# A conditioned transformer layer on one core: the output gate moved to the head of its slot, the first twelve attention slots taken by couples, and the inverse RMS spread through DRAM instead of by transpositions

## The reference, cut to what matters

```python
x = layernorm(x) * w + b + tanh(cond @ lin_w.T + lin_b)      # x: 128 sequences x 64 tokens x 256
x = x * w + b
rms = lambda v: v * rsqrt(mean(v * v, axis=-1) + 1e-6)
x = x + a_alpha * attention(a_gamma * rms(x) + a_beta)        # 16 heads of 16
h = f_gamma * rms(x) + f_beta
x = x + f_alpha * (silu(h @ gate_w.T) * (h @ hidden_w.T) @ out_w.T + out_b)   # hidden 1024
```

## Time and profile before

| | |
|---|---|
| median of 3 runs | 1007.26 us (1006.86 to 1007.68) |
| the profiled execution's own time | 1006.64 us |
| its span | 1004.8 us |
| TensorE busy | 943.0 us, 94% of the span |
| VectorE, ScalarE, GpSimd busy | 719.9, 623.0, 581.7 us |
| mean granted clock of TensorE | 0.993 |

### The profile page before, as it was taken

One profiled execution on the slowest core, in us unless ns is written; L12 is line 12 of the kernel. 1 busy time (PEld: TensorE's weight loads), 2 busy tenths in 40 slices (PEclk: granted clock), 3 DMA queues, 4 the chain that ended last, 5 costly groups with the idle time before them and its releaser, 6 DMA issues.

```text
span 1004.8 us, 28386 instructions
## 1 busy us (share of the span) xinstructions
PE 943.0 (94%) x11164; PEld 899.6 (90%) x11164; DVE 719.9 (72%) x1349; ACT 623.0 (62%) x1775; POOL 581.7 (58%) x531
## 2 busy tenths in 40 slices
PE   5566999999999999999999999999999999999998
PEld 5445899999999999999999999999999999999997
DVE  6656777777777777777777777777777776766655
ACT  4555766676566567656656765665667567666432
POOL 4556666757465665746566664656666565544320
PEclk9899999999999999999999999999999999999999
DMA  6000001000010100000010000001000000000000
GB/s 236 17 22 2 23 12 33 6 30 13 13 32 12 33 11 23 12 14 32 12 34 12 23 12 16 30 12 33 12 22 13 12 13 12 12 12 12 12 12 22
DMA packets 20931, 23.34 MB, mean 23 GB/s; under 512 B 1216, under 2 KB 20288, under 8 KB 20800
## 3 DMA queue, kind: packets, MB, share of 16 engines
q1 hardware_dynamic: 20800, 21.54, 6.6%
HBM read 13.15 MB, written 8.39 MB: 21 GB/s over the span
## 4 chain that ended last, share of the span: by engine, by line
PE 89%; DVE 4%; issue 3%; POOL 2%; ACT 1%; DMA 0%; SPq 0%; DVEq 0%; ACTq 0%; POOLq 0%
PE psum L293 18%; PE psum L295 17%; PE psum L294 17%; PE psum L507 6%; PE psum L506 6%; PE psum L505 6%; PE psum L432 5%; PE psum L408 4%; PE psum L448 4%; PE psum L342 2%; PE psum L323 2%; PE psum L501 1%; DVE late L721 1%; PE psum L331 1%; PE psum L335 1%
## 5 line engine op out<-in xcount | busy, mean ns | idle before, releaser
L293 PE MATMUL psum<-xf_hi,ffn_hi 128*128 128x256 f32 x1024 | 289.8, 283 | 2.3 <-ACT probsT L905 1.6
L295 PE MATMUL psum<-xf_hi,ffn_lo 128*128 128x256 f32 x1024 | 285.9, 279 | 0.0
L294 PE MATMUL psum<-xf_lo,ffn_hi 128*128 128x256 f32 x1024 | 285.8, 279 | 0.0
L897 ACT ACTIVATE probs<-psum,least 128x64 f32<-128x64 f32 x976 | 215.7, 354 | 56.6 <-DVE least L632 55.3
L293 PEld LDWEIGHTS psum<-xf_hi,ffn_hi 128*128 128x128 f32 x1024 | 192.2, 188 | 3.6 <-issue 2.6
L1091 POOL TENSOR_TENSOR probs<-probs,inv_sum 128x512 f32<-128x512 f32 x128 | 134.8, 1053 | 104.2 <-DVE inv_sum L653 103.4
L295 PEld LDWEIGHTS psum<-xf_hi,ffn_lo 128*128 128x128 f32 x1024 | 192.4, 188 | 0.0
L294 PEld LDWEIGHTS psum<-xf_lo,ffn_hi 128*128 128x128 f32 x1024 | 192.0, 187 | 0.0
L926 ACT ACTIVATE prod_hi<-late 128x512 fp32r<-128x512 f32 x128 | 83.9, 656 | 136.1 <-DVE late L711 135.9
L507 PE MATMUL psum<-prod_hi,ffn_lo 128*128 128x256 f32 x512 | 143.1, 280 | 0.0
L703 DVE SCALAR_TENSOR_TENSOR late<-tanh,psum 128x512 f32<-128x512 f32 x128 | 87.4, 683 | 77.7 <-ACT tanh L920 77.7
(11 more groups left out here) (106 smaller groups left out, 2217.9 us busy)
## 6 DMA issues: line engine op xcount, KB each, us to landing
out_t_dram<-x_res SPq DMA_DIRECT2D x31, 256.0 KB, 2.2
xin<-x_dram SPq DMA_DIRECT2D x15, 512.0 KB, 4.0
w_raw<-attn_w_dram SPq DMA_DIRECT2D x1, 1024.0 KB, 7.0
x_res<-gate_w_dram SPq DMA_DIRECT2D x1, 1024.0 KB, 9.6
late<-hidden_w_dram SPq DMA_DIRECT2D x1, 1024.0 KB, 11.6
w_raw<-out_w_dram SPq DMA_DIRECT2D x1, 1024.0 KB, 6.4
xin<-x_dram SPq DMA_DIRECT2D x2, 256.0 KB, 2.9
k_heads<-mod_w_dram SPq DMA_DIRECT2D x1, 320.0 KB, 4.7
```

Source lines behind the costliest of these rows:

```text
L293: pe.matmul(out, stat_hi, mov_hi, start=first, stop=False)
L294: pe.matmul(out, stat_hi, mov_lo, start=False, stop=False)
L295: return pe.matmul(out, stat_lo, mov_hi, start=False, stop=last)
L897: op = act.activation(probs[g % 2][:, h * SEQ:(h + 1) * SEQ], scores[g % 2][:, h // 2, h % 2], ACT.Exp, bias=least[g % 2][:, h:h + 1], sca ...
```

## The change

Three edits. **Output gate:** `gate_ffn` moves on VectorE from behind the sums and scalings of its slot S1 to its head, ahead of `mean_squares_out`. **Couples:** `wide(g)` now holds for odd sequences too, so in slots 0 to 11 VectorE centres both sequences of a couple and inverts both sums in the even slot, ScalarE takes two wide exponentials one after the other, and GpSimd normalises both at the head of the even slot. **Inverse RMS:** from group 3 (`ROWS_FROM`) on, `spread_inverses` is gone. SyncE stores `mean_sq` to a small DRAM tensor, waits for it, and loads it back with every partition getting the same row of up to 512 numbers (`send_inverses`); `scale_a` and `scale_f` read that row from SBUF, and `scale_f` goes first. `turn_squares` reads every second column, so that the row comes out in the order of the tokens.

```diff
+ROWS_FROM = FFN_AT // PSEQ
...
         def wide(g):
-            return g < FFN_AT and g % 2 == 0
+            return g < FFN_AT
...
+        def token_cols(grp, ap, i):
+            return ap[:].rearrange("p (t i) -> p i t", i=2)[:, i] if grp >= ROWS_FROM else ap[:, i * P:(i + 1) * P]
...
+            def send_inverses(grp):
+                which = slice(0 if is_part(grp + 2) else 1, 2 if is_part(grp - 2) else 1)
+                sp.wait_ge(inv_made, grp + 3)
+                sp.dma_start(inv_dram[grp % 2].rearrange("(w p i) -> p w i", w=2, i=2)[:, which],
+                             mean_sq[:].rearrange("p (w i) -> p w i", i=2)[:, which]).then_inc(inv_stored, 16)
+                if grp >= ROWS_FROM + 2:
+                    sp.wait_ge(scaled_a, min(grp + 1, NPART))
+                    sp.wait_ge(scaled_f, grp - 3)
+                sp.wait_ge(inv_stored, 16 * (grp - ROWS_FROM + 1))
+                cols = slice(which.start * PART, which.stop * PART)
+                sp.dma_start(inverse[grp % 2][:, cols], inv_dram[grp % 2:grp % 2 + 1, cols].partition_broadcast(P)
+                             ).then_inc(row_loaded, 16)
...
+                if s % PSEQ == 1 and s // PSEQ >= ROWS_FROM and is_group(s // PSEQ):
+                    send_inverses(s // PSEQ)
...
-                if j == 2 and is_part(grp + 2):
+                if j == 2 and grp < ROWS_FROM:
                     pe.wait_ge(scaled_a, grp + 3)
-                if j == 2 and is_part(grp - 2):
-                    pe.wait_ge(scaled_f, grp - 1)
+                    if is_part(grp - 2):
+                        pe.wait_ge(scaled_f, grp - 1)
...
-                if j == 2 and is_group(grp) and s >= 0:
+                if j == 2 and 0 <= grp < ROWS_FROM:
                     spread_inverses(grp)
...
+                if j == 1 and 0 <= grp - 4 < NPART - 1:
+                    gate_ffn(grp - 4)
+                if j == 1 and grp - 4 == NPART - 1:
+                    finish_last(grp - 4)
                 if j == 1 and is_group(grp):
                     mean_squares_out(grp)
...
+                    if s == 0:
+                        scale_a(1)
+                    for g in (s, s + 1):
+                        if is_seq(g) and wide(g):
+                            invert_sums(g)
...
                 if j == 0 and is_part(grp + 2):
                     make_residual(grp + 2)
+                if j == 2 and is_part(grp - 2):
+                    scale_f(grp - 2)
                 if j == 2 and s >= 0 and is_part(grp + 2):
                     scale_a(grp + 2)
-                if j == 2 and is_part(grp - 2):
-                    scale_f(grp - 2)
-                if is_seq(s):
+                if is_seq(s) and not wide(s):
                     invert_sums(s)
```

More of the change, by code:

```diff
@@ L136, in conditioned_block @@
         prod_lo = [sb(f"prod_lo{i}", [P, BLK], F32R) for i in range(2)]
+        inv_dram = nc.dram_tensor("inv_dram", [2, 2 * PART], F32).ap()
+        inverse = [sb(f"inverse{i}", [P, 2 * PART]) for i in range(2)]
         gated_f = late[:, 0:KT * PART].rearrange("p (k c) -> p k c", k=KT)
@@ L173, in conditioned_block @@
         out_mm, gated_f_made, y_made = sem("out_mm"), sem("gated_f_made"), sem("y_made")
+        inv_stored, row_loaded = sem("inv_stored"), sem("row_loaded")
         last_gated, last_made = sem("last_gated"), sem("last_made")
@@ L330, in turn_squares @@
                     for i in range(2):
-                        mm = pe.transpose(norm_bank[:, i * P:(i + 1) * P], square_sum_a[:, i * P:(i + 1) * P], ident[:])
+                        mm = pe.transpose(norm_bank[:, i * P:(i + 1) * P], token_cols(grp, square_sum_a, i), ident[:])
                 if is_part(grp - 2):
@@ L670, in mean_squares_out @@
                 dve.wait_ge(ms_mm, grp + 3)
-                if grp >= -1:
+                if grp > ROWS_FROM:
+                    dve.wait_ge(inv_stored, 16 * (grp - ROWS_FROM))
+                elif grp >= -1:
                     dve.wait_ge(inv_spread, grp + 2)
@@ L677, in mean_squares_out, with scale_by_rms @@
                 dve.tensor_scalar(mean_sq[:, cols], square_mean[:, cols], RMS_EPS, None, ALU.add).then_inc(ms_out, 1)
[L679 to L682, removed]
+            def scale_by_rms(normed, grp, cols):
+                if grp < ROWS_FROM:
+                    dve.wait_ge(inv_spread, grp + 3)
+                    row = norm_bank[:, cols]
+                else:
+                    dve.wait_ge(row_loaded, 16 * (grp - ROWS_FROM + 1))
+                    row = inverse[grp % 2][:, cols]
+                return dve.tensor_tensor(normed[:], normed[:], row.unsqueeze(1).broadcast_to([P, KT, PART]), ALU.mult)
             def scale_a(m):
-                dve.wait_ge(inv_spread, m + 1)
                 dve.wait_ge(gamma_a, m + 1)
-                scale_by_rms(normed_a, 0).then_inc(scaled_a, 1)
+                scale_by_rms(normed_a, m - 2, slice(0, PART)).then_inc(scaled_a, 1)
             def scale_f(m):
-                dve.wait_ge(inv_spread, m + 5)
                 dve.wait_ge(gamma_f, m + 1)
-                scale_by_rms(normed_f, PART).then_inc(scaled_f, 1)
+                scale_by_rms(normed_f, m + 2, slice(PART, 2 * PART)).then_inc(scaled_f, 1)
             def ffn_split_lo(m):
@@ L780, in _ @@
                                 centre(g)
+                    if s == 0:
[3 more added lines that the diff above has]
+                            invert_sums(g)
                 if s == FIRST_SLOT + 2:
                     scale_a(0)
-                if s == 0:
-                    scale_a(1)
                 if j == 0 and is_part(grp + 2):
                     make_residual(grp + 2)
+                if j == 2 and is_part(grp - 2):
+                    scale_f(grp - 2)
                 if j == 2 and s >= 0 and is_part(grp + 2):
                     scale_a(grp + 2)
-                if j == 2 and is_part(grp - 2):
-                    scale_f(grp - 2)
-                if is_seq(s):
+                if is_seq(s) and not wide(s):
                     invert_sums(s)
@@ L794, in _ @@
                     attended_lo(grp - 1)
-                if j == 1 and 0 <= grp - 4 < NPART - 1:
-                    gate_ffn(grp - 4)
-                if j == 1 and grp - 4 == NPART - 1:
-                    finish_last(grp - 4)
                 if j == 3 and is_part(grp - 1):
@@ L883, in score_minima_found @@
                 if wide(g):
-                    act.wait_ge(scores_read, g + 1)
+                    act.wait_ge(scores_read, g + 2)
             def exponentials(g):
@@ L979, in _ @@
                     exponentials(s)
+                    if wide(s + 1):
+                        exponentials(s + 1)
                 if s == 0:
@@ L1007, in _ @@
                     half_tanh(f)
-                if s % 2 == 0 and is_seq(s + 1):
+                if s % 2 == 0 and is_seq(s + 1) and not wide(s + 1):
                     exponentials(s + 1)
@@ L1110, in _ @@
                     apply_beta_a(1)
+                for g in (s, s + 1):
+                    if s % 2 == 0 and is_seq(g) and wide(g):
+                        normalise_probs(g)
+                if s == 0:
                     split_lo_a(1)
```

2 lines of the change are left out of this document (1 added, 1 removed).

## The result

The change makes the kernel slightly slower. Its median is 1011.92 us (1006.68 to 1015.48, 16 runs) against 1007.45 us of before (1005.09 to 1009.07, 16 runs) beside it; the ratio is 1.0043, interval 1.0029 to 1.0056. The forecast was 983.8. The profiled execution's span is 1010.1 us, its own time 1011.9.

A forecast was written before the change was run, and what follows sets the result against it. After about 100 us only TensorE's work and stops were taken to count. Gate -16.8, transpositions -7.0 and couples +0.3 gave -23.5, so 983.1 from the profiled 1006.64, and a median of 983.8 us; range 978 to 997.

The forecast's parts named there:

- Output gate, -16.8: End of S1: `down` no longer waits for the output gate, 28 x 0.60 = 16.8 us gained.
- +0.3 us, between -2 and +3: Couples in slots 0 to 11: gains and delays nearly cancel, +0.3 us, between -2 and +3.
- The end of slot 11 within 2 us: Sign for the couples: slot 11 ends within 2 us of before.
- 2.4 + 2.6 and 0.3, 5.3: Inverse's way through DRAM: two DMAs of 2.4 and 2.6 us plus 0.3 for three semaphores, 5.3 us.
- The upper bound of 8.1: Inverse's way through DRAM: estimate from above, each small piece twice as dear, 5.2 + 2.9 = 8.1 us.
- The point where lateness starts to cost, 6.8: Steady groups: both DMAs may take 6.8 us before TensorE stands still; about 7.0 in odd groups.
- rival C: Row too late: each us beyond 6.8 costs one in 27 groups, slower from 7.7; chance 0.05 below break-even, 0.11 above.
- The sign that was named: Forecast wrong if the wait for `inverse` exceeds 1.6 us; then TensorE waits for `att_lo` in S3.
- Transpositions, 7.0 of 11.6: Groups 3 to 33: 116 transpositions gone save 11.6 us of TensorE, of which 7.0 us arrive.
- The odd groups' chain: Minima, merges and VectorE work up to `turn_squares` in odd groups leave even groups' S2 gaining only some 0.05 us.
- The read with a stride at 0: `turn_squares` reading every second column: 0 or a doubling worth 12 us; taken as 0.
- The scalings from SBUF: Two SBUF operands beside GpSimd: at worst `scale_a` takes 1.76 us, 1.07 more, inside the 1.6 us slack.

The follow-up runs named there:

- gate_alone: The kernel before with only the output gate moved to the head of its slot: 989.11 us, ratio 0.9823.
- dram_alone: The kernel before with only the inverse RMS row through DRAM from group 3 on: 1010.27 us, ratio 1.0037.
- stale_row: gate_and_dram with each scaling using the previous group's row, so it never waits for its own (wrong results): 987.28 us, ratio 0.9807.
- gate_and_dram: The changed kernel without the couples (gate first, rows through DRAM): 1003.07 us, ratio 0.9967; run again on a third chip, 1002.65 us.
- hybrid: gate_and_dram with rows through DRAM only in groups 3 to 29, TensorE spreading inverses in groups 30 to 33: 997.68 us, ratio 0.9916.
- down_first: hybrid with scalings behind `att_lo`, statistics merges in S0 of odd groups, and `down` ahead of the values' projection in S2: 986.90 us, ratio 0.9792.
- the two runs on the second chip: gate_and_dram with the output's store moved to S3, 1011.68 us; gate_and_dram with the statistics merges moved to S0 of odd groups, 1007.38 us.

## Why the prediction was wrong

- **Output gate, -16.8: right.** gate_alone gave -17.6, and its cover, the idle time ahead of the mean squares, held.
- **"+0.3 us, between -2 and +3" for the couples: failed, it is +9.1.** I counted VectorE's order and let the rest follow. What stands behind two normalisations on GpSimd was given 1.9 us and only in slot 0; in slots 2, 6 and 10 the next part's beta stands there as well. The queries, priced as 2.2 late once and made good by probabilities ready earlier, wait 5.07 where they waited 2.77, and `att_lo` makes TensorE wait 4.28 instead of 2.44. "The end of slot 11 within 2 us" was 11.3. That the granted clock would fall with longer gaps was named and priced inside the +3; it went from 0.93 to 0.73 between 50 and 75 us.
- **"2.4 + 2.6 and 0.3, 5.3": failed, it is 7.3.** This is the largest miss: the late row that follows from it is 15 of the 28 us between forecast and result. The upper bound of 8.1 held. I chose the lower end because sizes didn't matter in the earlier trace rows, but each small piece did: 3.0 and 3.9 at the median. The Trainium skill (DMA: Bandwidth & Descriptors, section Anatomy of one DMA) gives a fixed 2.0 us and the bytes over 436 GB/s, measured on another path than SyncE's; an estimate by it is 2.0 + 2.6 for the two DMAs. The rows disagree, and the load takes 4.0 us for 128 KB and 3.9 for 256.
- **The point where lateness starts to cost, 6.8: about right, and rival C was what happened.** The way of 7.3 lies 0.5 beyond it; by C's rule that is 27 x 0.5 = 13.5 us, and 9.4 were lost in the steady part, since half of the groups lose nothing ahead of the output projection. In dram_alone, where the slot was still 0.6 longer, the same 7.3 cost nothing there, and the steady part was as before (758.36 against 758.23): what the transpositions might have given was used up as told below. The sign that was named, a wait of over 1.6 us for `inverse` and TensorE waiting for `att_lo` in S3, is what the rows show (62.4 / 31 = 2.0 us). What the count left out is that the lateness runs on behind `att_lo`: some 2.4 of the 9.8 us lie in S0 and S1 of odd groups. C had 0.11 for a way above its break-even of 7.7 and 0.05 for one below it, and 7.3 is below.
- **Transpositions, 7.0 of 11.6: mechanism right in part, size wrong, about 2.** The 2 are stale_row against gate_alone, 987.28 against 989.11, and their intervals overlap. The odd groups' chain exists, and it binds at `hidden` in S0 as well as at `turn_squares`. What I missed is that the values' projection waits for the copy of the turned probabilities: from stale_row against gate_alone, scores to values lose 0.21 of each 0.40 (27 x 0.21 = 5.7), queries 0.18 in odd groups (13 x 0.18 = 2.3), and the squares 0.05 in even groups and 0.10 in odd ones (2.0): 10.0 of 10.8. The largest of the three was not in the prediction.
- **The read with a stride at 0:** the squares of the even groups take 0.41 to the next product instead of 0.35, so at least that is not 0; 31 x 0.05 = 1.6 us, near the lower bound. The Trainium skill (SBUF — State Buffer, section Door 1) has such a stride free; the difference of 0.05 speaks against it, but no run took the stride alone away.
- **The scalings from SBUF:** `scale_f` took 691 to 694 ns in all 31 groups of gate_and_dram. `scale_a` started 0.16 us ahead of GpSimd's beta and took 681 to 689 ns, as forecast, while that beta took 1.42 us instead of 1.04.
- **The tail, "groups 30 to 33 pay half of 0.8": wrong sign.** hybrid puts the price of rows there at 5.5 us, and stale_row says that it is the wait.
- **The sum.** -17.6 for the gate, +9.1 for the couples, about -2 for the transpositions, +9.4 and +5.6 for the late row make +4.5, where -23.5 was forecast and +4.5 was measured. That the tenths agree is luck, as the terms come from different chips.

What stays open: why the product behind the moved `down` comes later in down_first, and why the way was 0.28 us longer in the two runs on the second chip.

## What to carry to other kernels

Price a detour by where its slack ends up, on every engine in the queue behind it, until an idle gap is found; two edits that spend the same slack cannot be added. Moving the instruction that waits only moves the lateness to whatever stands behind it, and runs are compared with runs on the same chip when tenths of a microsecond count 27 times. Removing TensorE work that lay over another engine's copy only uncovers the wait for that copy. When work is merged into couples, put what feeds the next stage ahead of what only has to be ready by the end of the couple.

## What the runs showed of the hardware

A 2 KB store to DRAM in 8-byte pieces took 2.5 to 4.5 us (median 3.0) until the load behind it could start, and a row read by all partitions 3.3 to 4.6 us (median 3.9), from the two lines' own views:

```profile
DMA to landing us min/median/max: 2.5/3.0/4.5
```

```profile
DMA to landing us min/median/max: 3.3/3.9/4.6
```

A 256 KB store issued right behind such a load landed in 4.1 us and in 2.1 when issued later. A stop of TensorE of 2.00 us in the tail was followed by 0.9 us at 2.4 GHz and 3.4 us at 1.2 GHz; in gate_and_dram a stop of 2.2 us in the same place was followed by no fall. A scaling with both inputs in SBUF took 0.68 us with a beta of GpSimd started 0.16 us behind it, and the beta took 1.42 us instead of 1.04.
